# A two-layer graph network on one core: chunks gathered ahead, the spread of the gathers, and the order of TensorE's work

## The reference

```
h = relu(layernorm(x))
# first layer: attention with a self loop on every node, four heads of 32
x_l, x_r = h @ W_l + b_l, h @ W_r + b_r
m     = leaky_relu(x_l[s] + x_r[d])            # s, d: the edges and one loop per node
e     = einsum(m, att); e = exp(e - segment_max(e, d)[d])
alpha = e / segment_sum(e, d)[d]
x     = x + segment_sum(alpha * x_l[s], d) + bias
# second layer: filtered messages
h     = relu(layernorm(x)) @ W_in2f
Wij   = (ssp(edge_attr @ Wf1 + bf1) @ Wf2 + bf2) * edge_weight
x     = x + ssp(segment_sum(h[src] * Wij, dst) @ Wo1 + bo1) @ Wo2 + bo2
```

## Time and profile before

| | |
|---|---|
| median of three runs | 3220.76 us (3219.39 to 3221.46) |
| the profiled execution | 3218.55 us, of which span 3216.6 |
| busy | PE 83%, DVE 82%, ACT 71%, POOL 60% of the span |
| mean granted clock of PE | 0.918 |

### The profile page before, as it was taken

One profiled execution on the slowest core, in us unless ns is written; L12 is line 12 of the kernel. 1 busy time (PEld: TensorE's weight loads), 2 busy tenths in 40 slices (PEclk: granted clock), 3 DMA queues, 4 the chain that ended last, 5 costly groups with the idle time before them and its releaser, 6 DMA issues.

```text
span 3216.6 us, 58243 instructions
## 1 busy us (share of the span) xinstructions
PE 2662.0 (83%) x16380; PEld 1753.5 (55%) x16380; DVE 2636.3 (82%) x6617; ACT 2281.9 (71%) x4803; POOL 1925.5 (60%) x1600
## 2 busy tenths in 40 slices
PE   6999988888988888876766888888888878858887
PEld 4666654444444444433333555555555556647776
DVE  7888869999999999966577888888888888747776
ACT  6999977777777777755555656666665656559998
POOL 2444447777777777765544888888888887810000
PEclk9999999999999999988887988889888988879999
DMA  6777743333333333322233665566665666679998
GB/s 244 283 278 280 282 164 131 118 130 111 116 130 117 132 117 131 116 101 80 88 95 92 118 126 117 116 117 120 123 119 117 116 116 118 122 293 422 422 422 354
DMA packets 266255, 546.17 MB, mean 170 GB/s; under 512 B 82836, under 2 KB 159092, under 8 KB 228450
## 3 DMA queue, kind: packets, MB, share of 16 engines
q1 hardware_dynamic: 171122, 441.98, 39.7%
q0 software_dynamic: 95024, 102.96, 16.2%
HBM read 317.77 MB, written 235.91 MB: 172 GB/s over the span
## 4 chain that ended last, share of the span: by engine, by line
issue 21%; DVE 20%; PE 19%; POOL 16%; ACT 15%; DMA 8%; SPq 1%; POOLq 0%; ACTq 0%; DVEq 0%
POOL sum_dram L608 8%; ACT d_n L1027 6%; PE bank L1404 3%; POOL x_dram L596 3%; PE bank L1214 3%; DMA sum_dram<-b_sum,b_at 3%; DVE a_max L826 2%; DVE f_ssp_out L978 2%; PE bank L1251 2%; POOL a_xs L549 2%; PE bank L1373 2%; DVE stat_e_six L804 2%; DVE stat_e_six L802 2%; DMA b_w<-weight_dram 2%; ACT turned L1024 2%
## 5 line engine op out<-in xcount | busy, mean ns | idle before, releaser
L608 POOL DMA_INDIRECT sum_dram<-b_sum,b_at x392 | 645.4, 1646 | 164.0 <-issue 108.3
L549 POOL DMA_INDIRECT a_xs<-in_x,index x392 | 391.4, 998 | 236.9 <-issue 154.1
L558 POOL DMA_INDIRECT a_xd<-in_x,index x392 | 384.8, 982 | 190.4 <-issue 116.6
L565 POOL DMA_INDIRECT x_dram<-a_xo,index x196 | 243.6, 1243 | 220.0 <-DVE a_xo L843 148.4
L1373 PE MATMUL bank<-b_rows,b_same 128*128 128x128 bf16 x4704 | 316.6, 234 | 0.0
L1373 PEld LDWEIGHTS bank<-b_rows,b_same 128*128 128x128 bf16 x4704 | 301.7, 106 | 0.0
L596 POOL DMA_INDIRECT x_dram<-b_xo,sidx x196 | 244.4, 1247 | 75.8 <-issue 57.0
L1027 ACT ACTIVATE d_n<-d_x,stat_d_shift,stat_d_rstd 128x128 f32<-128x128 f32 x686 | 283.4, 485 | 0.2 <-DVE stat_d_shift L644 0.2
L1404 PE MATMUL bank<-wo,f_ssp_out 128*128 128x128 f32 x1568 | 227.3, 288 | 55.2 <-DVE f_ssp_out L978 50.8
L1251 PE MATMUL bank<-wl,turned 128*128 128x128 f32 x1568 | 231.5, 292 | 41.0 <-ACT turned L1024 30.8
L978 DVE SCALAR_TENSOR_TENSOR f_ssp_out<-bank,cols,f_ln_out 128x512 f32<-128x512 f32 x196 | 147.1, 751 | 124.4 <-ACT f_ln_out L1199 106.4
(11 more groups left out here) (187 smaller groups left out, 7197.9 us busy)
## 6 DMA issues: line engine op xcount, KB each, us to landing
d_x<-in_x SPq DMA_DIRECT2D x49, 1024.0 KB, 6.9
x_dram<-d_x SPq DMA_DIRECT2D x49, 1024.0 KB
d_x<-x_dram SPq DMA_DIRECT2D x49, 1024.0 KB, 12.2
out<-d_x SPq DMA_DIRECT2D x49, 1024.0 KB, 8.5
sum_dram<-zero SPq DMA_DIRECT2D x48, 1024.0 KB, 5.8
d_n<-sum_dram SPq DMA_DIRECT2D x25, 1024.0 KB, 10.2
x_end_dram<-a_x SPq DMA_DIRECT2D x98, 256.0 KB, 3.6
b_x<-x_end_dram SPq DMA_DIRECT2D x98, 256.0 KB, 4.2
```

Source lines behind the costliest of these rows:

```text
L549: pool.indirect_dma_start(a_xs[t % DEPTH][:, j * F:(j + 1) * F], None, x, column(t, j)).then_inc(gathered[t % GSEM], 16)
L558: pool.indirect_dma_start(a_xd[t % DEPTH][:, j * F:(j + 1) * F], None, x, column(t, TILES + j)).then_inc(gathered[t % GSEM], 16)
L565: pool.indirect_dma_start(x1_dram, column(t, 2 * TILES + j), a_xo[s][:, j * F:(j + 1) * F], None, bounds_check=bound, oob_is_err=False).th ...
L608: pool.indirect_dma_start(sum_dram, bass.IndirectOffsetOnAxis(ap=b_at[s][:, j:j + 1], axis=0), b_sum[s][:, j * F:(j + 1) * F], None, compu ...
```

## The change

Four things.

1. Six chunks of the attention stage (30, 42, 54, 67, 79 and 91, the list `staged`) are gathered beside the dense stage. POOL gathers a chunk into the last pair of buffers, waits until it has landed, stores it to stage_dram, and waits for that before it takes the next. SP loads it into its usual buffers 20 steps before its own step. The 24 chunks kept in buffers follow in the same list `ahead`, whose 108 items are spread over the groups of the dense stage.
2. The rest of the gathers is spread evenly over the turns, `-(-len(rest) * (t + 1) // (NC - 8))`, without the term that held them at five chunks ahead.
3. a_base, its semaphores and its DVE add are gone. PE puts bias, a_hd @ wl and a_o @ ident into one bank, 6 or 7 by turns, two steps after the chunk's own; a_hd has three buffers for that, and a_xd is read by the x1 add. So a_xd is freed by `x1_ready`.
4. The turning of a_o, until now a transpose, is an ordinary product with ident that adds to the bank. It stands with the bias at the head of PE's step, ahead of a_nd's transposes.

```
+STAGED = 6
+        staged = [DEPTH + (2 * i + 1) * (NC - DEPTH) // (2 * STAGED) for i in range(STAGED)]
+        def landed(t):
+            return 128 * sum(u not in staged for u in range(t % GSEM, t + 1, GSEM))
...
+                if t + DEPTH - 4 in staged:
+                    g = t + DEPTH - 4
+                    i = staged.index(g)
+                    if i:
+                        sp.wait_ge(stage_loaded, 32 * i)
+                        sp.sem_inc(sync_step, 1)
+                    for sent in (norm_src, norm_dst, x1_ready):
+                        sp.wait_ge(sent, g - DEPTH + 1)
+                        sp.sem_inc(sync_step, 1)
+                    sp.dma_start(a_xs[g % DEPTH][:, :], stage_dram[i, 0, :, :]).then_inc(stage_loaded, 16)
+                    sp.dma_start(a_xd[g % DEPTH][:, :], stage_dram[i, 1, :, :]).then_inc(stage_loaded, 16)
...
-                    pool.wait_ge(base_ready, t - DEPTH + 1)
+                    pool.wait_ge(x1_ready, t - DEPTH + 1)
...
-            for t in range(DEPTH):
-                for n, gather in enumerate((gather_src, gather_dst)):
-                    pool.wait_ge(d_x1_ready, QUADS * min(RX + 1 + 2 * t + n, NG))
+            def gather_stage(i, h):
+                if h == 0 and i >= 1:
+                    pool.wait_ge(stage_stored, 32 * i)
+                    pool.sem_inc(pool_step, 1)
+                for j in (2 * h, 2 * h + 1):
+                    for rows, n in ((a_xs, 0), (a_xd, TILES)):
+                        pool.indirect_dma_start(rows[DEPTH - 1][:, j * F:(j + 1) * F], None, x, column(staged[i], n + j)).then_inc(stage_gathered, 16)
+                if h:
+                    pool.wait_ge(stage_gathered, 128 * (i + 1))
+                    pool.sem_inc(pool_step, 1)
+                    for n, rows in enumerate((a_xs, a_xd)):
+                        pool.dma_start(stage_dram[i, n, :, :], rows[DEPTH - 1][:, :]).then_inc(stage_stored, 16)
+            ahead = [(gather_stage, i, h) for i in range(STAGED) for h in range(2)]
+            ahead += [(gather, t, h) for t in range(DEPTH) for gather in (gather_src, gather_dst) for h in range(2)]
+            for n, (gather, t, h) in enumerate(ahead):
+                group = RX + 1 + n * (NG - RX - 3) // len(ahead)
+                if n == 0 or group != RX + 1 + (n - 1) * (NG - RX - 3) // len(ahead):
+                    pool.wait_ge(d_x1_ready, QUADS * group)
...
-                until = min(len(rest), max(-(-len(rest) * (t + 1) // NC), 4 * (t + 6 - DEPTH)))
+                until = min(len(rest), -(-len(rest) * (t + 1) // (NC - 8)))
...
-                    dve.tensor_tensor(a_x1[s][:, :], bank[7][:, :], a_base[s][:, :], ALU.add).then_inc(x1_ready, 1)
+                    dve.tensor_tensor(a_x1[s][:, :], bank[6 + s][:, :], a_xd[(t - 2) % DEPTH][:, :], ALU.add).then_inc(x1_ready, 1)
...
-                if front:
-                    dve.wait_ge(base_mm, t + 1)
-                    dve.tensor_tensor(a_base[s][:, :], bank[6][:, :], a_xd[t % DEPTH][:, :], ALU.add).then_inc(base_ready, 1)
...
+                if t >= 2:
+                    c = t - 2
+                    to = bank[6 + s]
+                    if c >= 2:
+                        pe.wait_ge(x1_ready, c - 1)
+                    pe.matmul(to[:, :], ones3[:, 0:P], bias3[:, :, :].rearrange("k j f -> k (j f)"), start=True, stop=False)
+                    for j in range(TILES):
+                        pe.matmul(to[:, j * F:(j + 1) * F], a_hd[c % 3][:, j * P:(j + 1) * P], wl[:, :], start=False, stop=False)
+                    pe.wait_ge(att_out, c + 1)
+                    for j in range(TILES):
+                        last = pe.matmul(to[:, j * F:(j + 1) * F], a_o[s][:, j * P:(j + 1) * P], ident[:, :],
+                                         start=False, stop=(j == TILES - 1))
+                    last.then_inc(out_turned, 1)
                 if front:
                     pe.wait_ge(norm_dst, t + 1)
                     turn_tiles(bank[1], a_nd).then_inc(turned_dst, 1)
```

More of the change, by code:

```diff
@@ L151, in gnn @@
         a_hs = sb("a_hs", [P, C])
-        a_hd = sb("a_hd", [P, C])
+        a_hd = [sb(f"a_hd{i}", [P, C]) for i in range(3)]
         a_us = sb("a_us", [P, C])
@@ L170, in gnn @@
         a_o = two("a_o", [P, C])
-        a_base = two("a_base", [P, TILES * F])
         a_x1 = two("a_x1", [P, TILES * F])
@@ L263, in gnn @@
         den_all = sem("den_all"); den_log = sem("den_log"); den_rec = sem("den_rec")
-        base_ready = sem("base_ready"); att_out = sem("att_out"); out_turned = sem("out_turned")
+        att_out = sem("att_out"); out_turned = sem("out_turned")
         x1_ready = sem("x1_ready"); early_ready = sem("early_ready")
@@ L384, in _ @@
                 sp.sem_inc(sync_step, 1)
+            sp.wait_ge(stage_stored, 32 * STAGED)
+            sp.sem_inc(sync_step, 1)
             for t in range(NC + 3):
@@ L542, in gather_src @@
                     if t >= GSEM:
-                        pool.wait_ge(gathered[t % GSEM], 128 * (t // GSEM))
+                        pool.wait_ge(gathered[t % GSEM], landed(t - GSEM))
                         pool.sem_inc(pool_step, 1)
@@ L566, in early_scatters @@
                                             bounds_check=bound, oob_is_err=False).then_inc(early_scattered[s], 16)
-            for t in range(DEPTH):
-                for n, gather in enumerate((gather_src, gather_dst)):
-                    pool.wait_ge(d_x1_ready, QUADS * min(RX + 1 + 2 * t + n, NG))
+            def gather_stage(i, h):
+                if h == 0 and i >= 1:
+                    pool.wait_ge(stage_stored, 32 * i)
                     pool.sem_inc(pool_step, 1)
-                    for h in range(2):
-                        gather(t, h)
+                for j in (2 * h, 2 * h + 1):
[13 more added lines that the diff above has]
+                    pool.sem_inc(pool_step, 1)
+                if n == 2 * STAGED:
+                    pool.wait_ge(stage_stored, 32 * STAGED)
+                    pool.sem_inc(pool_step, 1)
+                gather(t, h)
             for i in range(RN):
@@ L576, in _ @@
                 pool.sem_inc(pool_step, 1)
-            rest = [(gather, t, h) for t in range(DEPTH, NC) for gather in (gather_src, gather_dst) for h in range(2)]
+            rest = [(gather, t, h) for t in range(DEPTH, NC) if t not in staged for gather in (gather_src, gather_dst) for h in range(2)]
             done = 0
@@ L799, in sums_a @@
                 n = t % 2 * 2 * TILES
-                dve.wait_ge(gathered[t % GSEM], 128 * (t // GSEM + 1))
+                if t in staged:
+                    dve.wait_ge(stage_loaded, 32 * (staged.index(t) + 1))
+                else:
+                    dve.wait_ge(gathered[t % GSEM], landed(t))
                 for j in range(TILES):
@@ L1075, in step_a @@
                     act.wait_ge(turned_dst, t + 1)
-                    act.activation(a_hd[:, :], bank[1][:, :], ACT.Relu).then_inc(h_dst, 1)
+                    act.activation(a_hd[t % 3][:, :], bank[1][:, :], ACT.Relu).then_inc(h_dst, 1)
                 if mid:
@@ L1289, in step_a @@
                     turn_tiles(bank[1], a_nd).then_inc(turned_dst, 1)
-                if t >= 2:
-                    pe.wait_ge(att_out, t - 1)
-                    if t >= 3:
-                        pe.wait_ge(x1_ready, t - 2)
-                    turn_tiles(bank[7], a_o[s]).then_inc(out_turned, 1)
-                if front:
-                    if t >= 1:
-                        pe.wait_ge(base_ready, t)
-                    pe.matmul(bank[6][:, :], ones3[:, 0:P], bias3[:, :, :].rearrange("k j f -> k (j f)"), start=True, stop=False)
+                    hd = a_hd[t % 3]
                     pe.wait_ge(h_dst, t + 1)
-                    for j in range(TILES):
-                        last = pe.matmul(bank[6][:, j * F:(j + 1) * F], a_hd[:, j * P:(j + 1) * P], wl[:, :],
-                                         start=False, stop=(j == TILES - 1))
-                    last.then_inc(base_mm, 1)
                     if t >= 1:
                         pe.wait_ge(edge_relu, t)
-                    pe.matmul(bank[2][:, :], wlr[:, :], a_hd[:, :], start=True, stop=True).then_inc(self_mm, 1)
-                    pe.matmul(bank[3][:, :], neg_wl[:, :], a_hd[:, :], start=True, stop=False)
+                    pe.matmul(bank[2][:, :], wlr[:, :], hd[:, :], start=True, stop=True).then_inc(self_mm, 1)
+                    pe.matmul(bank[3][:, :], neg_wl[:, :], hd[:, :], start=True, stop=False)
                     pe.matmul(bank[3][:, :], wl[:, :], a_hs[:, :], start=False, stop=True).then_inc(v_mm, 1)
                     pe.matmul(bank[4][:, :], wl[:, :], a_hs[:, :], start=True, stop=False)
-                    pe.matmul(bank[4][:, :], wr[:, :], a_hd[:, :], start=False, stop=True).then_inc(edge_mm, 1)
+                    pe.matmul(bank[4][:, :], wr[:, :], hd[:, :], start=False, stop=True).then_inc(edge_mm, 1)
                     if t >= 1:
```

6 lines of the change are left out of this document (3 added, 3 removed).

## The result

The changed kernel takes 3063.45 us (3062.11 to 3063.78; the kernel before, run beside it, 3220.07): a ratio of 0.9513, with a 95% interval of 0.9496 to 0.9529. On a second chip it took 3062.16, ratio 0.9521 [0.9502, 0.9539]. The forecast was 3087, with a range of 3064 to 3135: the measured time lies 23 us under the one and just outside the other. The slow end went, PE became the bound and waits for a_hd, as forecast; what was mispriced is POOL's turn, and with it the pace. The profiled execution took 3062.11 us, of which span 3060.1.

The account below looks back on a forecast made before the run. Bound by DVE for 78 attention steps, then by POOL and DVE waiting for each other for 19; -135 (-88 gathers, -47 pace of 11.2) and +1 staging give -134: 3087 us, range 3064 to 3135.

Parts of the forecast that it names:

- (1): Attention stage: even gathers end the POOL-DVE loop, so the 19 slow steps take the others' pace, -88 us.
- (2): Attention stage: two DVE operations become one, so DVE's step falls to 10.34 and 11.07 us, mean 10.7.
- (3): Attention stage: PE's new order gives a loop of 11.05 us, about 0.75 of it a bare wait for a_hd.
- (4): Attention stage: POOL's turn of 6.04 gathers and 2 scatters takes 11.05 to 11.4 us; pace taken as 11.2.
- The clock: Attention stage: few half-clock stretches expected, since PE would be busy about 10.3 of 11.2 us.
- Rival A: Attention stage: half-clock stretches stay as frequent, 11.6 us a step, -97 us, 3124; chance 0.20.
- (5): Dense stage: staging takes POOL 115 to 140 us, through at 195 to 220, almost all hidden, +1 us.
- rival E: Dense stage pays 10 to 20 us for the staging, 3097 to 3107; chance 0.04.
- (6): SP's 12 loads of 256 KB, 18 DVE steps ahead of use, cost 0.
- Rival B: Attention stage: PE's loop is longer because att_out or ACT comes late, pace about 12.1 us, 3173; chance 0.08.
- C: Attention stage: the lead is eaten and the last chunks still wait for gathers, 3147; chance 0.05.
- D: Attention stage: slower, PE without slack at a clock of 0.86, 12.85 us a step, +25 us, 3246; chance 0.03.

Follow-up runs that it names:

- gathers alone: Kernel before plus staging and even gathers only, with a_base, its add and PE's order as before: 3124.85 us against 3218.33, ratio 0.9705.
- less work on PE: Changed kernel with x1 leaving out the bias and a_hd @ wl, nine products a step: 3039.33 us, ratio 0.9419.
- no staging: Changed kernel without the six staged chunks, all 74 gathered in the attention stage, 6.58 gathers a turn: 3107.74 us, ratio 0.9662.

## Why the prediction was off by 23 us

(1) *Even gathers*: right. -88 said, -93.5 measured by "gathers alone"; in the changed kernel the pace does not change at t = 77.

(2) *DVE's step*: right. 10.34 and 11.07 said, 10.35 and 11.05 measured once PE was out of the way.

(3) *PE's loop*: right. 11.05 said, 11.00 measured; the bare wait for a_hd is 0.69 for 0.75 said.

(4) *POOL's turn*: the step that failed. "6.04 x 1.318 + 2 x 1.70 = 11.4 us ... With a gather's 0.305 in its place the turn is 11.05", and from that a pace of 11.2. A turn of the changed kernel's 6.04 gathers costs POOL some 10.8: with six it takes 10.79 on the average in "less work on PE" and 10.78 in "no staging", where POOL does not wait for DVE. With POOL under PE the pace is PE's own: 97 x (11.2 - 10.96) = 23 us, which is the error. Some 15 of them are the way from 11.2 down to PE's 11.05, the other 9 are the 0.09 by which PE's pace came out under the walk.

What made the price too high is above all the scatter: its 1.241 us was a mean over turns most of which begin with a wait. In the kernel before 68 of 77 turns begin with more than 0.35 us of idle; the second scatter of these takes 1.45 us on the average (34 of them over 1.3), and 1.06 in the other nine. A single one, from the turn of the earlier trace rows that begins with a wait of 4.47 us:

```profile
1452.36 1.91 POOL L565 DMA_INDIRECT x_dram<-a_xo,index  x1 [0.30 <-issue]
```

Where POOL does not wait, scatters take 1.07 ("no staging") and 1.09 ("less work on PE"), with 0.30 in front of each. I took out the idle above 0.305 and left what the waits had put into the duration. That the waiting lengthens them is an inference from these turns; no run changes it alone, and in "less work on PE" 16 of 83 second scatters take over 1.3 us with no wait before them.

The prediction also said that a turn 0.3 us shorter would move the sum by nothing, since PE's 11.05 is then the bound. But the sum stood on 11.2, not on 11.05, so it would have moved by 97 x 0.15 = 15 us. And the comparison there of gathers of 0.95 us beside a waiting DVE with 1.013 beside a busy one does not hold: in the changed kernel gathers of 0.94 and 0.95 stand beside a DVE that works without a pause (1007.18 and 1008.43 us).

*The clock*: better than said. "Few half-clock stretches" was argued from PE's busy share; there was none from 480 us to 1530, and the clock of 1.00 in "less work on PE", with PE busy less than in "gathers alone", shows that the share is not the reason. So the term came out right by luck as much as by argument. Rival A (3124) fell by the clock of 1.00. "Gathers alone" keeps 0.97, so what spared the changed kernel lies in parts 3 and 4; that part 3 alone would have left rival A right is not shown, as no run has it without part 4.

(5) *The staging*: through at 229 us, not 195 to 220, since a store took 8.7 us to land and not one to two gathers' time, and the last gathers' landing 5.8 and not 3.3. It cost nothing: the kept chunks' gathers were over at 470 (435 to 460 said), still 11 us ahead of the first scatter, which waits for DVE. The dense stage was said to pay +1 and paid -1.2, with the DMA engines busy 0.85 for 0.78. So the 22 us of the engines' interleaving and rival E are not seen here.

(6) *SP's loads*: 0, as said; no wait names them.

Rival B (late att_out or ACT) fell: from 480 to 1391 us nobody waits for att_out. C fell: there is no wait for gathers. D fell: the clock rose. E is answered under (5). The range's lower end rested on PE's 11.05 a step (3072) and some wandering of the other stages; the measured time lies 0.55 us under it, and PE's pace of 10.96 in place of 11.05 is 9 us. That PE stands bare for ACT's a_hd while DVE waits for the score product was half right: DVE's slack shows in front of a_o, at ACT's a_rec (23.4 us).

## What to carry to other kernels

Price an engine's turn from a place where it works without standing still, not from means: here scatters in turns that began with a wait had a longer mean than those in turns without one. A kernel in which three engines lie within 5% pays only for the longest, so the gain of one edit is cut at the next engine's own loop; a run that takes work off one engine alone tells both numbers. And of two halves of a change, count what each allows the other, in the stage where they act: they gave 150 us apart and 159 together there.

## What was not expected of the hardware

- The granted clock rose from 0.97 to 1.00 when four transposes of 128x128 a step became eight passes of ordinary products, though that is 0.46 us more work on PE a step; and it stayed at 1.00 with PE 14% idle ("less work on PE").
- Two stores of 256 KB to DRAM, issued by POOL beside 1 MB transfers, had landed 8.7 us after the issue, and the last gathers 5.8 to 6.2, where the median of this gather had been 3.3.
- On three chips every kernel took 4 to 13% longer than elsewhere, with stops of up to 35 us that no instruction of the program explains; the last dense stage ran there at full rate (423 GB/s).
